# Aggregation tiles of layer 1 in clusters of three behind whole expert products

## The reference

```python
def _rgcn_conv(x, edge_index, edge_type, basis, comp, root, bias):
    W = jnp.einsum('rb,bde->rde', comp, basis)       # 8 relations from 4 bases
    h = jnp.einsum('nd,rde->nre', x, W)
    msg = h[src, edge_type]
    seg = dst * R + edge_type
    sums = jax.ops.segment_sum(msg, seg, num_segments=n * R)
    cnt = jax.ops.segment_sum(ones, seg, num_segments=n * R)
    mean = sums / jnp.maximum(cnt, 1.0)[:, None]
    return mean.reshape(n, R, -1).sum(axis=1) + x @ root + bias
# gnn
h = relu(_rgcn_conv(layernorm(x), ..., basis0, comp0, root0, bias0))
h = relu(_rgcn_conv(h, ..., basis1, comp1, root1, bias1))
x = x + (h @ lin_w[node_type] + lin_b[node_type])
# ffn, on layernorm(x) normed again with gamma, beta
logits = xn @ Wr + br;  top 2, softmax -> w_full
for e in range(8):
    y = y + (gelu(xn @ W1[e] + b1[e]) @ W2[e] + b2[e]) * w_full[..., e]
x = x + y
```

## Time and profile before

| | |
|---|---|
| median of 3 runs | 4837.2 us |
| profiled execution | 4840.02 us, span 4838.2 us |
| PE busy, weight loads | 3842.3 us (79%), 3300.8 us (68%) |
| VectorE, GpSimd, ScalarE busy | 3017.5, 3331.7, 881.8 us |
| mean clock of TensorE | 0.78 of full |
| L1251, tiles' matmuls | 21168, 1380.1 us busy |
| L1338, up; L1351, down | 867.1 us; 842.0 us |

### The profile page before, as it was taken

How to read it: one execution, slowest core, us unless ns; L and a number is a source line. 1 busy time by engine, 2 the same in 40 slices (tenths; PEclk the granted TensorE clock), 3 DMA queues, 4 the chain that set the end, 5 groups by cost and what they waited for, 6 DMA issues and landing times.

```text
span 4838.2 us, 119647 instructions
## 1 busy us (share of the span) xinstructions
PE 3842.3 (79%) x38119; PEld 3300.8 (68%) x38120; DVE 3017.5 (62%) x6579; ACT 881.8 (18%) x2470; POOL 3331.7 (69%) x3374
## 2 busy tenths in 40 slices
PE   1366666666666666666469999999999999999999
PEld 1255555555555555555358888888888888888888
DVE  4556656666666566666456666666666666666663
ACT  1200000000000000000013333333333333333333
POOL 0477777777777777777477676767676777676770
PEclk6555555555555555555569999999999999999999
DMA  4656655555555555555465555555555555555551
GB/s 129 192 171 183 176 158 156 157 158 158 155 157 159 156 157 158 158 156 157 117 169 166 156 159 155 158 154 158 154 158 156 158 157 160 154 160 154 159 158 22
DMA packets 344661, 749.10 MB, mean 155 GB/s; under 512 B 128323, under 2 KB 167806, under 8 KB 344430
## 3 DMA queue, kind: packets, MB, share of 16 engines
q0 software_dynamic: 215040, 662.09, 48.7%
q1 hardware_dynamic: 115510, 70.49, 5.6%
q10 hardware_dynamic: 14076, 16.04, 1.0%
HBM read 719.00 MB, written 29.35 MB: 155 GB/s over the span
## 4 chain that ended last, share of the span: by engine, by line
PE 59%; issue 12%; DVE 12%; POOL 9%; DMA 8%; DVEq 0%; SPq 0%; ACT 0%; POOLq 0%; ACTq 0%
PE bank L1351 15%; PE bank L1338 14%; PE bank L1251 11%; POOL slot L558 9%; PE bank L1283 8%; DMA slot<-table,idx 6%; DVE inv L939 4%; PE bank L1247 3%; DVE scaled L945 3%; PE bank L1311 3%; PE bank L1312 2%; DVE mixed L913 2%; PE bank L1279 1%; DVE inv L938 1%; PE bank L1314 1%
## 5 line engine op out<-in xcount | busy, mean ns | idle before, releaser
L558 POOL DMA_INDIRECT slot<-table,idx x3354 | 3326.0, 992 | 1342.0 <-issue 1085.2
L1251 PE MATMUL bank<-hot,slot 128*128 (+1 forms) x21168 | 1380.1, 212 | 67.5 <-DMA slot<-table,idx 60.6
L1251 PEld LDWEIGHTS bank<-hot,slot 128*128 128x128 bf16 x21168 | 1112.1, 108 | 219.4 <-issue 75.0
L1247 PE MATMUL bank<-hot,ones_b 128*128 x1764 | 398.7, 226 | 745.4 <-DMA slot<-table,idx 340.1
L1338 PE MATMUL bank<-xnT,ffn_w 128*128 128x128 f32 x6272 | 867.1, 285 | 20.0 <-DVE scaled L945 20.0
L1247 PEld LDWEIGHTS bank<-hot,ones_b 128*128 128x128 bf16 x1764 | 181.0, 103 | 1006.4 <-issue 969.2
L1351 PE MATMUL bank<-ffn_w,act 128*128 128x256 f32 x3136 | 842.0, 395 | 0.3 <-DVE o L1024 0.3
L1338 PEld LDWEIGHTS bank<-xnT,ffn_w 128*128 128x128 f32 x6272 | 755.8, 192 | 46.4 <-DVE scaled L945 28.8
L1351 PEld LDWEIGHTS bank<-ffn_w,act 128*128 128x128 f32 x3136 | 541.1, 191 | 60.7 <-issue 16.9
L913 DVE SCALAR_TENSOR_TENSOR mixed<-scaled,small,mixed 128x256 f32<-128x256 f32 x1372 | 573.7, 480 | 12.2
L913 DVE SCALAR_TENSOR_TENSOR mixed<-scaled,comp_sb,mixed 128x256 f32<-128x256 f32 x1372 | 573.5, 480 | 10.5
(11 more groups left out here) (148 smaller groups left out, 2192.0 us busy)
## 6 DMA issues: line engine op xcount, KB each, us to landing
slot<-table,idx POOLq DMA_INDIRECT x3354, 3.1
inv<-inv_d SPq DMA_DIRECT2D x98, 256.0 KB, 3.8
table<-ffn_w SPq DMA_DIRECT2D x7, 1344.0 KB, 6.0
table<-parts ACTq DMA_DIRECT2D x49, 192.0 KB, 3.1
ffn_w<-in_L_ffn_W_dram SPq DMA_DIRECT2D x16, 512.0 KB
xcur<-in_x_dram SPq DMA_DIRECT2D x48, 128.0 KB
out_dram<-o ACTq DMA_DIRECT2D x48, 128.0 KB
ffn_w<-in_x_dram SPq DMA_DIRECT2D x6, 896.0 KB, 9.0
```

Of the source, the lines that this page charges most:

```text
L558: gp.indirect_dma_start(out=slot[:, k, :], out_offset=None, in_=table[layer], in_offset=bass.IndirectOffsetOnAxis(ap=idx[:, h, k:k + 1], a ...
L1247: t.matmul(C[:, at], ones_b[:, :], oh, start=(k == 0), stop=(k == TILES - 1), skip_group_check=True)
L1251: last = t.matmul(S[f][:, at], slot[:, k, q * D + f * P:q * D + (f + 1) * P], oh, start=(k == 0 and q == 0), stop=(k == TILES - 1 and q == ...
```

## The change

The two helpers lose their tiles between the halves; tiles follow a whole expert product, three at a time. The counts of each block stay 18: y gets 6 clusters (ups 1, downs 0, ups 2, downs 1, after typed product 2, ups 3), x gets 6 (ups 5, downs 4, ups 6, downs 5, ups 7, downs 6). Downs 2 and downs 7 have no tiles now. Nothing else of the kernel differs.

```diff
-                def ups(e, tiles=(0, 0)):
-                    for half in range(2):
-                        if r is not None:
-                            up(r, e, half)
-                        more(tiles[half])
-
-                def downs(e, tiles=(0, 0)):
-                    for half in range(2):
-                        if r is not None:
-                            down(r, e, half, a)
-                        more(tiles[half])
+                def ups(e, tiles=0):
+                    if r is not None:
+                        up(r, e, 0)
+                        up(r, e, 1)
+                    more(tiles)
+
+                def downs(e, tiles=0):
+                    if r is not None:
+                        down(r, e, 0, a)
+                        down(r, e, 1, a)
+                    more(tiles)
...
-                ups(1, (1, 2))
+                ups(1, RUN)
                 if a is not None:
                     transform(1, a + PAIRS, a)
-                downs(0, (1, 1))
-                ups(2, (1, 1))
-                downs(1, (1, 1))
+                downs(0, RUN)
+                ups(2, RUN)
+                downs(1, RUN)
                 for j in range(TYPES + 1):
                     if a is not None:
                         typed(a, j, r)
-                    if j < TYPES:
-                        more(1)
-                ups(3, (1, 1))
-                downs(2, (1, 1))
+                    if j == TYPES // 2:
+                        more(RUN)
+                ups(3, RUN)
+                downs(2)
...
-                ups(5, (1, 2))
-                downs(4, (1, 2))
-                ups(6, (1, 2))
+                ups(5, RUN)
+                downs(4, RUN)
+                ups(6, RUN)
...
-                downs(5, (1, 2))
-                ups(7, (1, 1))
+                downs(5, RUN)
+                ups(7, RUN)
...
-                downs(6, (1, 1))
-                downs(7, (1, 1))
+                downs(6, RUN)
+                downs(7)
```

## The result

The changed kernel takes 4805.55 us, the median of 4 runs (4804.79 to 4807.05), against 4838.03 (4836.73 to 4839.07): a ratio of 0.9934, interval 0.9922 to 0.9947. The kernel before has one more run here than in the table ahead of the change, hence 4838.03 and not 4837.2. That is 32 us less; 4809 was forecast.

What follows compares the result with a forecast made beforehand. Layer 1's x part was taken as bound by VectorE, its y part by PE. Saving 0.80 less a 0.20 stall gives 0.60 us per period, times 47 is 28 us: 4809 us, range 4790 to 4831.

Steps and rivals of the forecast that it cites:

- The two parts and their limits: Layer 1's period: x part, 19.81 us, limited by VectorE; y part, 28.30 us, limited by PE, falling to 27.7.
- 0.08 us per entry, ten of them: y part: each fp32 product after a bf16 tile starts 0.08 us slow; ten such starts go, saving 0.80 us a period.
- The entry before the typed bias: y part, weight load of 5 rows (L1314): the eleventh removed entry, counted at nothing; 0.08 us at its other end.
- The late cluster among the typed products: y part: PE's sequencer stands at product 2's wait, the three tiles behind it are fed late; stall about 0.20 us.
- Sum: Whole loop: 0.80 - 0.20 = 0.60 us per period, 47 times, 28 us in all.
- The other clusters of y are covered: Other five clusters of y: the sequencer runs ahead, a whole expert before each covers its feeding; no cost taken.
- The last tile of x, 1.7 us sooner, is worth nothing: x part: the tile now stands before downs 7, but earlier VectorE work keeps `scaled` from starting sooner; no gain.
- rival A: x part: VectorE isn't its limit, `scaled` waited for x's last tile; 1.23 us more in 46 periods, 4752; 7%.
- Rival B: Typed products: VectorE round trips cost three cold starts, leaving 0.2 us a period or nothing, 4828 to 4837; 10%.
- Rival C: All six y clusters: the sequencer is late, so the kernel is slower, 4856 at the least price; 6%.
- its dear form: One wholly uncovered tile in each y cluster, 0.88 us instead of 0.175: 3.4 a period, near 5000; 1%.
- The 62 ns a matmul with hardware decode off: Skill page's sequencer cost: a cluster of 18 would take 1.1 us, not 0.53, and the change would lose.

Runs made afterwards that it cites:

- run with VectorE shortened: Changed kernel with the sums of expert 6 and b2 moved behind the scaling of x's block on VectorE; 4747.77 us, ratio 0.9814 to the kernel before.
- the run with six: Changed kernel with tiles 6 to 11 of y in one cluster behind ups 2, none behind downs 1; 4837.67 us, ratio 0.9999 to the kernel before.
- the move in the kernel before: Kernel before, old tile order, with expert 6's and b2's sums put behind the scaling of x's block on VectorE; 4833.59 us, ratio 0.9991.

## Why the prediction was right

- *The two parts and their limits*: right. y 28.30 to 27.64 (27.7 said), x 19.81 to 19.80 (19.8 said), and PE's loss at expert 1 from 0.59 to 1.24 us from start to start (about 1.2 said), 0.43 to 1.07 of it marked idle. The run with VectorE shortened shows it and doesn't only argue it.
- *0.08 us per entry, ten of them*: right. It measures 1.81 - 1.73 and 1.86 - 1.78 on whole products. The single records of the changed kernel give 0.083 (1.867 and 1.784, 1.810 and 1.729). Ten are 0.83, where I had 0.80. The entry before the typed bias was rightly left at nothing; the bias product starts 0.09 late behind a full fp32 product (0.52 us pass before it where 0.43 is usual), as it did behind a tile (0.27 instead of 0.17).
- *The late cluster among the typed products*: right in place and cause, 0.15 instead of 0.20.
- *Sum*: 0.83 - 0.15 = 0.68 by these, 0.66 by the windows, against 0.60 forecast. 47 passes make 31 us of the span's 33.0 (4838.2 to 4805.2). Of the rest, 1.5 us is there already at the 15000th matmul (2406.8 against 2405.3), ahead of all that was edited, so it isn't the change's. Both terms were mis-sized by a little to the same side, and that makes most of the 3 us between 4809 and 4805.55.
- *The other clusters of y are covered*: right for three tiles (0.53 throughout). The reason was half right. I counted the product's time as cover; what protects a cluster is that it is no longer than the queue, as the run with six shows.
- *The last tile of x, 1.7 us sooner, is worth nothing*: right for this kernel, and only because VectorE's run ends later; rival A's mechanism was real and stood 0.10 us behind, as the move in the kernel before shows. The prediction had no number for this margin.
- *Rival B*: out, product 2 follows product 1 after the usual 0.43 (3518.51 to 3518.94).
- *Rival C*: out for three tiles, and its dear form was priced too high. The tiles 0.88 us apart ran at a granted clock of 0.50 (2460 to 2464 us), the lower of the two levels; at the full one the run with six has uncovered tiles 0.43 apart.
- *The 62 ns a matmul with hardware decode off*, from the Trainium skill, "TensorE: Matmul & The Clock Gate", section "Wait — 56ns, not 53.3ns?": not the mode here. 18 matmuls take 0.52 us, 29 ns each, though up to 17 of them had been issued before. The run with six settles it: there a tile's four register instructions and six matmuls together take the sequencer 0.43 us, and six times 62 ns would be 0.37 (an estimate from that figure) with the register instructions, 0.1 each, still to come. Nor does the figure alone make the change lose, as the prediction has it, for the same matmuls are issued before and after.

## What to carry to other kernels

Cut a period at its waits and ask of each part which engine ends it: the same edit gave 0.66 us in one part and nothing in the other, until a move on another engine made room there and the two together gave 1.2 us more than the sum of what each gives alone. In this kernel small bf16 matmuls are worth grouping between large fp32 ones, up to about the length of PE's queue (three tiles, 18 matmuls, cost nothing extra; six cost the whole gain), and not behind a wait at which the sequencer has to stand. When a stall goes nowhere although its engine got faster, look for a second chain that ends at the same semaphore.

## What the runs showed of the hardware

- The first fp32 matmul behind bf16 ones costs 0.083 us more, at either row length (128 and 256 columns: 1.867 against 1.784 us, 1.810 against 1.729). The other direction costs nothing that shows: a tile takes 0.174 us behind fp32, a third of the 0.524 of three. Why the entry costs this was not tried.
- PE's sequencer runs ahead by 17 matmuls with their weight loads (the word load at 3529.3 in the run with six, before). Its register instructions come 0.1 us apart; a tile of 6 matmuls with four of them needs 0.43 us, one with a word load 0.69 (3529.29 to 3529.99), while PE executes it in 0.175.
- Two chips ran the unchanged kernel in 6031 and 6033 us instead of 4838. The trace of one of its variants there has stalls of up to 2.8 us before matmuls, marked "issue", mostly at fixed places of the loop, and a granted clock of 0.91 in layer 1. The cause of the stalls wasn't tried.
